# Four attention blocks on one core: another order of the work between score bursts, and tile normalisation and squares on ScalarE

## What is computed

```python
x = x + squared(layernorm(x))   # q, k = layernorm per head of (Wq x, Wk x) * gamma + beta; weights (q.k)^2, divided by their sum
x = x + gated(layernorm(x))     # a gate picks one head's k and v for each token, shared by all heads; softmax
x = x + mqa(layernorm(x))       # one k and one v head, biases, output projection; softmax
x = x + gated(layernorm(x))
```

## Time and profile before

| | |
|---|---|
| median of 3 runs | 4739.77 us (4738.4 to 4744.24) |
| the profiled execution | 4741.89 us |
| its span, first to last instruction | 4740.1 us |
| TensorE (PE) matmul busy | 3849.7 us, 81% |
| GpSimd (POOL) busy | 2991.2 us, 63% |
| VectorE (DVE) busy | 1899.4 us, 40% |
| ScalarE (ACT) busy | 1630.1 us, 34% |
| mean granted TensorE clock | 0.918 |

### The profile page before, as it was taken

The page is one execution under the profiler, slowest core; times in us unless marked ns, Lnnn a source line. Parts: engine busy times, 40 slices in busy tenths (PEclk is TensorE's granted clock), DMA queues, the critical chain, the costliest instruction groups (busy, mean ns, idle before and its releaser), DMA issues. The chain is left out here.

```text
span 4740.1 us, 66857 instructions
## 1 busy us (share of the span) xinstructions
PE 3849.7 (81%) x26018; PEld 1585.2 (33%) x26018; DVE 1899.4 (40%) x4874; ACT 1630.1 (34%) x2433; POOL 2991.2 (63%) x2215
## 2 busy tenths in 40 slices
PE   6788888985978688688786888888798886977975
PEld 4343434322333233233232333333333332323332
DVE  1212212222544444444444445444544444544452
ACT  1543444551223223323333333333233233232333
POOL 2967777983254646547676676776557466465587
PEclk9899998987989889899898999999899997988998
DMA  1001010003000100100101010010001001010010
GB/s 62 18 1 37 18 36 19 19 19 103 18 1 1 54 1 8 48 1 21 34 17 38 1 34 21 23 32 25 30 1 54 1 19 36 1 53 2 1 37 27
DMA packets 63382, 115.05 MB, mean 24 GB/s; under 512 B 8672, under 2 KB 9184, under 8 KB 63072
## 3 DMA queue, kind: packets, MB, share of 16 engines
q1 hardware_dynamic: 63072, 110.77, 7.2%
HBM read 77.19 MB, written 33.55 MB: 23 GB/s over the span
## 5 line engine op out<-in xcount | busy, mean ns | idle before, releaser
L775 ACT ACTIVATE probs_soft<-banks 128x1024 f32<-128x1024 f32 (+1 forms) x960 | 848.6, 936 | 1426.0 <-PE banks L1078 1411.1
L688 POOL TENSOR_TENSOR added_soft<-added_soft,probs_soft 128x2048 f32<-128x2048 f32 (+3 forms) x384 | 1163.9, 3031 | 67.0 <-ACT probs_soft L775 47.9
L867 DVE CUSTOM_DVE_ANT_0 banks<-banks,mask 128x128 f32<-128x128 f32 (+3 forms) x1536 | 700.7, 525 | 739.1 <-PE banks L1093 739.1
L862 DVE TENSOR_REDUCE maxima_soft<-banks 128x2 f32<-128x1024 f32 x384 | 452.4, 1221 | 527.1 <-PE banks L1093 527.1
L1093 PE MATMUL banks<-k_soft,q_soft 32*128 32x512 f32 (+3 forms) x4608 | 531.4, 555 | 140.4 <-ACT probs_soft L775 140.3
L781 ACT ACTIVATE probs_squared<-banks,key_scale_squared 128x512 f32<-128x512 f32 (+3 forms) x768 | 379.2, 590 | 382.5 <-PE banks L1078 371.6
L665 POOL TENSOR_SCALAR_AFFINE_SELECT probs_soft<-probs_soft 128x512 f32<-128x512 f32 x384 | 239.7, 637 | 427.7 <-ACT probs_soft L775 427.6
L1078 PE MATMUL banks<-q_soft,k_soft 32*128 32x512 f32 (+3 forms) x4608 | 505.7, 521 | 0.0
L1131 PE MATMUL banks<-probs_soft,v_soft 128*32 128x512 f32 (+3 forms) x4608 | 454.2, 514 | 46.0 <-POOL probs_soft L665 31.7
L688 POOL TENSOR_TENSOR added_squared<-added_squared,probs_squared 128x2048 f32<-128x2048 f32 (+3 forms) x128 | 390.2, 3048 | 7.3 <-ACT probs_squared L781 1.9
L1075 PE MATMUL banks<-shift_soft,ones 32*128 32x512 bf16 (+3 forms) x2304 | 205.4, 344 | 227.2 <-DVE maxima_soft L867 136.4
(11 more groups left out here) (153 smaller groups left out, 4801.0 us busy)
## 6 DMA issues: line engine op xcount, KB each, us to landing
tiles_soft<-out SPq DMA_DIRECT2D x96, 256.0 KB, 2.9
rest_soft<-out SPq DMA_DIRECT2D x96, 256.0 KB, 3.0
out<-rest_soft SPq DMA_DIRECT2D x96, 256.0 KB, 2.1
tiles_squared<-in_x SPq DMA_DIRECT2D x32, 256.0 KB, 2.9
rest_squared<-in_x SPq DMA_DIRECT2D x32, 256.0 KB, 3.2
out<-rest_squared SPq DMA_DIRECT2D x32, 256.0 KB, 2.0
raw_wq<-in_squared_wq SPq DMA_DIRECT2D x1, 1024.0 KB, 5.6
raw_wk<-in_squared_wk SPq DMA_DIRECT2D x1, 1024.0 KB, 7.9
```

The lines of the kernel that those rows point to most:

```text
L688: ins = pool.tensor_tensor(sums, sums, slot(ph, n)[:, :, col:col + width], ALU.add)
L775: ins = act.activation(slot(ph, n)[:, 2 * a:2 * a + 2, 0:width], score_pair(e, a)[:, :, 0:width], ACT.Exp, scale=SCALE)
L862: ins = dve.reduce_max(m["maxima"][:, ph % 2, 2 * a:2 * a + 2, t, p], score_pair(e, a)[:, :, col:col + width], AX_X)
L867: ins = dve.tensor_tensor_reduce(scores, scores, k["mask"][:, CHUNK - width:CHUNK], 1.0, MASKED, ALU.add, ALU.max, m["maxima"][:, ph % 2, ...
```

## The change

**The order.** Free work is cut into single products (`PIECES`; `v2` into two) instead of halves, and `av` into four parts. A half's share of the free work is in proportion to `KEYS_TAKEN` or `ROWS_TAKEN`, a table of how long its burst occupies the engine that empties the scores, instead of the same for each half; the bursts' own TensorE weight no longer counts. `since` says when free work may start. The first four loads of the next stage stand at the very start of a stage; its normalisation (`steps`) is laid between this stage's output tiles and then between the first products of the next stage's keys and values, which may now begin as soon as normalised tiles are there. Keys come before queries in `features`; the `gt`, `gtt`, `gate` chain has query projections in between.

**Normalisation.** GpSimd makes `rstd` and, new, `norm_shift` = -mean x rstd (128x1). ScalarE then normalises the tile in place by one Identity activation with scale and bias (a new event `norm`, in its list behind the preceding tile's `ln`). **Squares** of keys and queries (`ksq`, `qsq`) are made by ScalarE.

```diff
-HALVED = ("av", "q", "q2", "k2", "v2", "ks", "kall", "vall")
+PIECES = {"av": 4, "q": KC, "q2": KC, "k2": KC, "v2": 2, "ks": KC, "kall": KC, "vall": KC}
+KEYS_TAKEN = {512: 1.25, 256: 0.85}
+ROWS_TAKEN = {P * n: (masked, plain) for n, masked, plain in ((1, 0.95, 0.4), (2, 1.2, 0.65), (3, 1.45, 0.95), (4, 1.75, 1.25))}
...
-def norm_events(s):
-    events = [("stats", s, t) for t in range(3)]
+def norm_events(s, between):
+    head = [("load", s, t) for t in range(TILES)], [("stats", s, t) for t in range(TILES)] + [("norm", s, 0)]
+    steps = []
     for t in range(NT):
-        if t + 3 < NT:
-            events.append(("stats", s, t + 3))
-        events.append(("ln", s, t))
-        if t + TILES < NT:
-            events.append(("load", s, t + TILES))
-    return events
+        steps.append([("ln", s, t)] + [("load", s, t + TILES)] * (t + TILES < NT))
+        if t >= 2 and t + 2 < NT:
+            steps[-1].append(("stats", s, t + 2))
+        steps[-1] += [("norm", s, t + 1)] * (t + 1 < NT)
+    between = [between[n::NT] for n in range(NT)] if len(between) > NT else [between[n:n + 1] for n in range(NT)]
+    return head, [steps[t] + between[t] for t in range(NT)]
...
 def features(ph):
-    return [(u, ph, c) for c in range(NC) for u in ("q2", "k2", "ksq")] + [("kvar", ph, c) for c in range(NC)]
+    return [(u, ph, c) for us in (("k2", "ksq"), ("q2",)) for c in range(NC) for u in us] + [("kvar", ph, c) for c in range(NC)]
...
-        first = [("gt", s, 0), ("gt", s, 1), ("gtt", s, 0), ("gtt", s, 1), ("gate", s), ("gate_exp", s), ("gate_value", s)]
+        first = [("gt", s, 1), ("gtt", s, 0), queries[0][0], ("gtt", s, 1), ("gate", s), ("gate_exp", s), queries[0][1], ("gate_value", s)]
         first += [("kall", s, t) for t in range(NT)]
         first.insert(len(first) - 2, ("krep", s, 0))
-        first += [("krep", s, 1), ("kt", s, 0)] + queries[0] + [("kt", s, 1)]
-        return first, [("vall", s, t) for t in range(NT)] + queries[1]
-    first = [("ks", s, 0), ("ks", s, 1)] + queries[0] + [("vs", s, 0), ("vs", s, 1), ("vst", s, 0), ("vst", s, 1)]
-    return first, queries[1]
+        first += [("krep", s, 1), queries[1][0], ("kt", s, 0), queries[1][1], ("kt", s, 1)]
+        return [("gt", s, 0)], first, [("vall", s, t) for t in range(NT)]
+    first = [("ks", s, 1), ("vs", s, 1), ("vst", s, 0), queries[0][1], ("vst", s, 1)] + queries[1]
+    return [("ks", s, 0), ("vs", s, 0), queries[0][0]], first, []
...
+def taken(n):
+    return sum(ROWS_TAKEN[P * blocks][0 if p == t // TPC else 1] for t, p, blocks, col in ROW_BURSTS[n]) + 0.15
...
+    room = [KEYS_TAKEN[sum(p[2] for p in KEY_BURSTS[h // 2][2])] for h in range(HALVES)]
...
+            room[2 * k + 1] = taken(k)
...
-        at[h].append(("more", ("av", of, part)))
-        at[h + 1].append(("av", of, part))
+        at[h] += [("more", ("av", of, part))] * 2
+        at[h + 1] += [("more", ("av", of, part)), ("av", of, part)]
...
-    fixed = [sum(weight(e, kinds) for e in h) for h in halves]
-    queue = [(e, since, until) for part, since, until in work for e in in_halves(part, kinds)]
...
+def since(event):
+    event = event[1] if event[0] == "more" else event
+    if event[0] in ("q", "q2", "k2"):
+        return (event[1] % NG + 1) * HALVES if event[1] % NG < 2 else 0
+    if event[0] == "v2":
+        return 2 * HALVES + 3 if event[2] else 3
+    return 0
+def spread(kinds, halves, rooms, work):
+    fixed = [sum(weight(e, kinds) for e in h if e[0] not in ("keys", "rows")) for h in halves]
+    queue = [(e, since(e), until) for part, until in work for e in in_pieces(part, kinds)]
...
-            pace = max(pace, (ahead + sum(fixed[n:until])) / (until - n))
-        room = carry + pace - fixed[n]
+            pace = max(pace, (ahead + sum(fixed[n:until])) / sum(rooms[n:until]))
+        room = carry + pace * rooms[n] - fixed[n]
...
+            between, first, rest = keys_and_values(kinds[s + 1], s + 1)
+            head, steps = norm_events(s + 1, [])
+            behind = outs[half:]
+            merged = []
+            for t in range(NT // 2):
+                of = next((n for n, e in enumerate(behind) if e[0] == "out"), len(behind) - 1) + 1
+                merged += steps[t] + behind[:of]
+                behind = behind[of:]
+            merged += behind
+            later = []
+            for t in range(NT // 2):
+                later += between[t:t + 1] + steps[NT // 2 + t]
+            later += between[NT // 2:]
...
+            own = [features(4 * s + 2), features(4 * s + 3)]
+            work = [(head[0], 1), (outs[:half], 2 * HALVES - 2), (own[0], 2 * HALVES - 2), (own[1], 3 * HALVES - 2),
+                    (head[1], 2 * HALVES + 6), (merged, 2 * HALVES + 6)]
         else:
-            queries = [[("q", 4 * s + g, c) for c in range(NC)] for g in (2, 3)]
-            work = [(queries[0], 0, HALVES - 2), (outs[:half], 0, 2 * HALVES - 2), (queries[1], 0, 2 * HALVES - 2),
-                    (outs[half:], 0, 2 * HALVES + 6)]
-        if s + 1 < stages:
-            first, rest = keys_and_values(kinds[s + 1], s + 1)
-            work.append(([("load", s + 1, t) for t in range(TILES)] + norm_events(s + 1), 0, NG * HALVES))
-            work.append((first + rest, 2 * HALVES + 5, NG * HALVES))
-        events += spread(kinds, halves, work)
+            own = [[("q", 4 * s + g, c) for c in range(NC)] for g in (2, 3)]
+            work = [(head[0], 1), (own[0], HALVES - 2), (outs[:half], 2 * HALVES - 2), (head[1], 2 * HALVES - 2),
+                    (own[1], 2 * HALVES - 2), (merged, 2 * HALVES + 6)]
+        work.append((later + first + rest, NG * HALVES))
+        events += spread(kinds, halves, rooms, work)
...
                     pool.wait_ge(sg.variance, place[e] + 1)
+                    if s:
+                        pool.wait_ge(sg.normed, NT * (s - 1) + t + 1)
                     then(pool.tensor_tensor(m["rstd"][:, t:t + 1], m["var_eps"][:, t:t + 1], k["minus_half"][:, 0:1], ALU.pow))
-                    x = m["tiles"][:, t % TILES, :]
-                    pool.tensor_scalar(x, x, m["minus_mean"][:, t:t + 1], m["rstd"][:, t:t + 1], ALU.add,
-                                       ALU.mult).then_inc(sg.normed, 1)
+                    pool.tensor_tensor(m["norm_shift"][:, t:t + 1], m["minus_mean"][:, t:t + 1], m["rstd"][:, t:t + 1], ALU.mult)\
+                        .then_inc(sg.scaled, 1)
...
-                elif u == "ksq":
-                    _, ph, c = e
-                    wait_free(pool, ("k2", ph, c))
-                    if ph:
-                        wait_work(pool, ("kvar", ph - 1, c))
-                    keys = k_of(ph)[:, CHUNK * c:CHUNK * c + CHUNK]
-                    pool.tensor_tensor(m["key_square"][:, c], keys, keys, ALU.mult).then_inc(sg.key_squares, 1)
-                elif u == "qsq":
-                    _, ph, c = e
-                    wait_free(pool, ("q2", ph, c))
-                    if ph:
-                        wait_work(pool, ("sm", ph - 1, c))
-                    queries = m["q"][:, ph % NG, CHUNK * c:CHUNK * c + CHUNK]
-                    pool.tensor_tensor(m["query_square"][:, c], queries, queries, ALU.mult).then_inc(sg.query_squares, 1)
...
+                elif u == "norm":
+                    _, s, t = e
+                    act.wait_ge(sg.scaled, place["stats", s, t] + 1)
+                    x = m["tiles"][:, t % TILES, :]
+                    act.activation(x, x, ACT.Identity, scale=m["rstd"][:, t:t + 1], bias=m["norm_shift"][:, t:t + 1])\
+                        .then_inc(sg.normed, 1)
+                elif u == "ksq":
+                    _, ph, c = e
+                    wait_free(act, ("k2", ph, c))
+                    if ph:
+                        wait_work(act, ("kvar", ph - 1, c))
+                    act.activation(m["key_square"][:, c], k_of(ph)[:, CHUNK * c:CHUNK * c + CHUNK], ACT.Square)\
+                        .then_inc(sg.key_squares, 1)
+                elif u == "qsq":
+                    _, ph, c = e
+                    wait_free(act, ("q2", ph, c))
+                    if ph:
+                        wait_work(act, ("sm", ph - 1, c))
+                    act.activation(m["query_square"][:, c], m["q"][:, ph % NG, CHUNK * c:CHUNK * c + CHUNK], ACT.Square)\
+                        .then_inc(sg.query_squares, 1)
...
-            begun = set()
+            begun = {}
             def share(terms, e, opening):
-                terms = list(enumerate(terms))
+                terms, done = list(enumerate(terms)), begun.get(e, 0)
                 if opening:
-                    begun.add(e)
-                    return terms[:len(terms) // 2]
-                return terms[len(terms) // 2:] if e in begun else terms
+                    begun[e] = done + 1
+                    return terms[done:done + 1]
+                return terms[done:]
```

51 lines of the change are left out of this document (30 added, 21 removed).

## The result

The changed kernel takes **4543 us** (median of four runs, 4536.9 to 4546.7) against 4740 us before: a ratio of 0.9583, 95% interval 0.9566 to 0.9599. It is faster, as forecast, but by 197 us where 490 were forecast, and outside the range, whose upper end was 4490.

The account below looks back on a forecast made before the run. TensorE was taken to bound the kernel, with 890 us idle and a mean clock of 0.918. Stages, mostly at 0.95 x TensorE busy + 28 us, plus start, special stages and 1.8 us gave 4250 us; range 4080 to 4490.

Parts of the forecast that it names:

- the sum: Whole kernel: stages mostly at 0.95 x TensorE busy time + 28 us idle, plus start and special stages; 4250 us.
- all bounds of the terms at once: Whole kernel: every term at its end together would give 4022 or 4770 us.
- the clock's own bound: TensorE's clock: between nothing and 342 us given back; 210 us was estimated.
- TensorE's instructions are the same in number and size; only their places change.: TensorE's free work: the `g_wk` block's 32 products spread in pieces of one to four, with no added instructions.
- That is 8 us a stage instead of 34.0.: TensorE idleness at the normalisation: 4 us at the first tile plus 1 us at each of four; bounds 0 and 34.0.
- ScalarE held: Rival at the normalisation: TensorE's 231 us of waits for GpSimd return through ScalarE's queue; 4481 us, chance 0.12.
- The slower rival: Every `norm` of stages 2 to 16 holds ScalarE 4.5 us, and TensorE behind it; 4792 us, chance 0.05.
- I take back 5%, a factor of 0.95 on all busy time.: TensorE's clock: evenly loaded phases return to the high level; 210 us, 5.5% of busy time, estimated.
- I take 5, 20 us a stage.: TensorE idle time left per phase with work behind its bursts: 5 us, bounds 2.2 and 7.7.
- The floor of 55 us a phase: Lightly loaded phases: 55 us taken as the least time a phase can need.
- under half of 351 us: TensorE at the score banks: waits for maxima and probabilities, 351 us before, should fall below half.
- The sign named for failure: ScalarE's waits for `norm_shift` come to several us each, with TensorE's score waits growing behind them.

Follow-up runs that it names:

- Halves: The changed kernel with every product sum cut in two halves, as before the change, instead of into single products: 4424 us, ratio 0.9333.
- the third buffer: The changed kernel with three buffers instead of two for `scaled_out`, the scaled gated outputs: 4543 us, ratio 0.9580.
- The outputs in a lump: Tested on the changed kernel by raising the planner's weight of a gated output from 0.9 to 2.7, so that outputs stand apart: 4472 us, ratio 0.9435.
- the best kernel: The changed kernel with sums cut in halves, first normalisation early, gated outputs apart and normalisation on GpSimd, squares staying on ScalarE: 4302 us, ratio 0.9080.
- first normalisation early: The changed kernel with the next stage's first four tile statistics and first `norm` put ahead of the gated outputs: 4508 us, ratio 0.9510.
- 92 groups more in the old order: The kernel before, its order kept, with sums cut into single products as in the change: 4841 us, ratio 1.0213.

## Why the prediction was wrong

**The direction and what bounds the kernel** were right: TensorE bounds it, and the new order brings the gain. Each cost that I put at nothing or at little was too low.

**The miss in the terms of the sum.** Over the 64 phases the sum has some 0.95 x 3770 = 3582 us of busy time and 551 of idle time. Measured are 3746 and 680. So 164 of the 293 us that it missed lie in the factor on the busy time (42 us of work that the change added, and 122 us that the clock did not give back), and 129 in the idle time, most of which the sum has as 20 and 8 us a stage. Either part alone would have stayed under 4490. What the prediction calls "all bounds of the terms at once" takes only the idle terms; with the clock's own bound, nothing given back, its upper end of 4770 would be some 190 us higher. The steps, one by one:

*"TensorE's instructions are the same in number and size; only their places change."* This step failed. The places are the cost: 304 more groups, for 42 us more work at the full clock, and sums that end inside a burst with their bank held behind VectorE's maxima. Halves remove 120 us of the 293 that the forecast missed. I priced the portions only by TensorE's own time and at nothing for their beginnings, and took no account of who has to read a sum, although shows VectorE behind the score banks.

*"That is 8 us a stage instead of 34.0."* GpSimd's chain before the first `rstd` I had at 10.7 us; the timeline has 1778.50 to 1788.68, 10.2 us. What it does to TensorE I had at 4 us, "less what the ring holds"; it was 4.44 + 4.89 = 9.3 us in this phase (the 3.06 us ahead of them belong to the row maxima). Two things were missing. VectorE stands too: its reads of the outputs wait for the same chain, and the statistics are queued behind them. And TensorE had the outputs, but they need VectorE; the third buffer showed that without this hold TensorE waits 10.27 us for ScalarE instead. The outputs in a lump are worth 71 us, which the prediction does not look at; the planner gives an output a small weight. The normalisation on ScalarE costs 60 us against its being on GpSimd. It also takes 812 ns a tile, not the 690 that I took:

```profile
L820 ACT ACTIVATE tiles_soft<-tiles_soft,norm_shift_soft,rstd_soft 128x512 f32<-128x512 f32 x96 | 78.0, 812 | 256.9 <-POOL norm_shift_soft L702 256.8
...
L834 ACT ACTIVATE query_square_squared<-q_squared 128x512 f32<-128x512 f32 x32 | 20.6, 645 | 0.0
```

That is 0.12 x 128 = 15 us of ScalarE, which is idle 61% of the time, so it cannot make the 60; what costs is the place in its queue, as the timeline shows it. The rival "ScalarE held" (4481 us) had this mechanism, but took it for the only one and put it at 231 us; it is 60. The slower rival, 4.5 us of standing at each of 120 tiles, fell: ScalarE waited at 28 of the 96 tiles of the second act, not at each. The Trainium skill's page "Perfetto Trace Analysis", section "Tensor Engine Instruction (MATMUL, LD_WEIGHTS)", calls ScalarE a strict first-in first-out engine; the trace agrees, with the exponentials at 1790.25 behind a `norm` that had waited 16.51 us.

*"I take back 5%, a factor of 0.95 on all busy time."* This is the largest single term of the miss. 329 us of busy time in the phases lie at the low level (480 before), so the clock gave back (480 - 329) x 0.44 = 66 us, not the 188 of the sum. The low clock stands where the stalls stand: 0.86 in the first phase, 1.00 in the third. The mechanism was right and its size was not: the stalls that I had at little stayed, and the clock with them. With the stalls reduced, in the best kernel, 227 us lie at the low level, which is 111 us given back. The Trainium skill's page "TensorE: Matmul & The Clock Gate", section "HAM oscillation — how this bites in real kernels", prices low-clock time at half its length. The trace does not agree for this kernel: 258 us of low time left the phases (759 to 501), and 66 us came of it, not 129.

*"I take 5, 20 us a stage."* It holds where nothing else interferes: 6.5 and 6.4 us in the last two phases after, 4.2 and 4.4 with halves. The floor of 55 us a phase holds in the changed kernel: the last phases of the four stages that prepare an mqa stage take 56.1, 55.2, 56.4 and 56.4. It is no fixed floor, since with halves the first two of them take 53.9 and 53.5. But the waits at the banks did not fall to under half of 351 us (203, and 246 in the best kernel). The squares were likely right in sign: `kvar`'s 52.2 us of waits for GpSimd went, and they bring 11 to 16 us.

Of what the new profile was to show, one point held: from the first gated stage on TensorE has no idle time over 10 us, 7.0 at most ahead of the last stage and 9.4 in it. Four failed: phases within 10 us of each other (86.2 to 67.7), the transposes' waits under 100 us (147), busy time near 3650 at a clock over 0.95 (3824 at 0.942), and the bank waits. The sign named for failure, ScalarE waiting for `norm_shift` several us at a time, is there: 28 times, 257 us.

In sum, the change's 4543 us less 120 (cutting), 71 (lump), 60 (normalisation) and 35 (first normalisation early) would be 4257; the best kernel has all four and measured 4302, so they overlap by 45 us. The last 50 us between it and the forecast of 4250 are open. Its bank waits, 246 us, are the largest candidate, but no run took those away.

## What to carry to other kernels

When filler work for the bounding engine is cut finer, count what each piece costs at its beginning, and ask who must read its result before the bank comes free: a sum should end where its reader is idle. Weigh every event of a planner by the slowest engine that it occupies, not by its time on the bounding one; the gated outputs, weighed 0.9 for TensorE but followed by 1.3 us of GpSimd behind its adds, show it. And before moving work from a loaded engine to one that is idle most of the time, ask whether its inputs come from an engine that is behind: here the normalisation, fed by GpSimd, lost 60 us, and the squares, made from what ScalarE itself had just written, gained 11 to 16.

## What the runs showed of the hardware

A piece of a product sum cost TensorE 0.19 us beyond its products by the timelines (1.05, 1.91 and 3.63 us for one, two and four products at the full clock). The totals, which are estimates and take in whatever else the orders differ in, give 0.22 us with 92 groups more in the old order, 0.25 with 121 fewer in the new one, and 0.14 for the 304 that the change added. ScalarE's activation on 128x512 took 812 ns with scale and bias both given per partition and the tile written in place, 640 as a square, and 600 as a copy out of a bank.
